# One power for rows of x1 and scale of u, and a new order of steps on GpSimd and VectorE

## The reference

```python
xn = layernorm(x)
x1 = x + gnn(xn, edges) + mix(xn)      # gnn: softmax over 4 heads, gathered rows; mix: attention in a hyperbolic ball
y  = x1 + ffn(layernorm(x1))           # ffn: a router picks 2 of 8 experts for all rows, then layernorm
# mix, per block of rows, where one batch row makes each attention its own position:
#   t = relu(bn(xn @ w_qkv)), s = pointwise(t), q, k = relu, v; out = (v k) q / (v + 1e-15)
#   scaled by norms of t, s and out; u = out @ w_res + b; fx = tanh(|u|) u / |u|, clipped at the ball's edge
```

## Time and profile before

| | |
|---|---|
| time, median of 3 runs | 835.66 us (833.97 to 837.52) |
| profiled execution, its own time | 833.71 us |
| its span | 831.9 us |
| attention stage with its tail, 218 to 486 us | 268.0 us |
| TensorE busy, share of the span | 94% |
| VectorE / ScalarE / GpSimd busy | 63% / 51% / 46% |

### The profile page before, as it was taken

How to read it: one execution, slowest core, us unless ns; L and a number is a source line. 1 busy time by engine, 2 the same in 40 slices (tenths; PEclk the granted TensorE clock), 3 DMA queues, 4 the chain that set the end, 5 groups by cost and what they waited for, 6 DMA issues and landing times. The chain is left out here.

```text
span 831.9 us, 15073 instructions
## 1 busy us (share of the span) xinstructions
PE 780.0 (94%) x5042; PEld 639.1 (77%) x5042; DVE 525.7 (63%) x1480; ACT 424.9 (51%) x963; POOL 384.8 (46%) x601
## 2 busy tenths in 40 slices
PE   5899999999798999999669899999999999999996
PEld 3778888888466666666446788888888888888885
DVE  6863488797578888888988635353535353535345
ACT  2566436889679888888657242323222222223230
POOL 2430878878068888877646502221213131313122
PEclk9999999999999999999979999999999999999999
DMA  9855122222011110211100040000000000000000
GB/s 216 208 146 148 43 57 57 51 57 52 8 50 47 51 59 25 63 45 53 41 10 30 20 126 14 26 13 25 13 25 13 25 12 25 16 23 17 22 20 30
DMA packets 35420, 41.31 MB, mean 50 GB/s; under 512 B 11520, under 2 KB 20696, under 8 KB 35339
## 3 DMA queue, kind: packets, MB, share of 16 engines
q1 hardware_dynamic: 22355, 30.71, 12.9%
q0 software_dynamic: 8000, 6.82, 3.8%
q10 hardware_dynamic: 4984, 2.79, 1.4%
HBM read 25.59 MB, written 14.60 MB: 48 GB/s over the span
## 5 line engine op out<-in xcount | busy, mean ns | idle before, releaser
L926 ACT ACTIVATE Z<-ps,b1s 128x250 f32<-128x250 f32 x200 | 93.5, 469 | 233.1 <-PE ps L1195 233.1
L1208 PE MATMUL ps<-Z 128*125 128x256 f32 x800 | 176.5, 379 | 0.0
L1195 PE MATMUL ps<-Z 128*128 128x250 f32 x800 | 173.3, 374 | 0.4 <-DMA Z<-in_w 0.4
L1208 PEld LDWEIGHTS ps<-Z 128*125 128x125 f32 x800 | 150.1, 188 | 22.3
L1195 PEld LDWEIGHTS ps<-Z 128*128 128x128 f32 x800 | 151.4, 189 | 18.3 <-DMA Z<-in_w 0.6
L988 PE MATMUL ps<-Z,L 128*128 128x250 f32 x600 | 126.9, 373 | 0.0
L655 POOL TENSOR_SCALAR zr<-zmv 125x1 f32<-125x1 f32 x50 | 11.1, 221 | 249.2 <-issue 239.9
L988 PEld LDWEIGHTS ps<-Z,L 128*128 128x128 f32 x600 | 113.6, 189 | 13.2
L1794 DVE TENSOR_TENSOR Z<-ps,L 125x256 f32<-125x256 f32 x50 | 21.2, 424 | 160.2 <-PE ps L1208 159.9
L1110 PE MATMUL ps<-wr,Z 128*125 128x256 f32 x400 | 92.6, 384 | 0.0
L780 ACT ACTIVATE Z<-Z,bn_o,bn_s 128x250 f32<-128x250 f32 x150 | 80.7, 598 | 1.5 <-DVE bn_o L1495 1.5
(11 more groups left out here) (221 smaller groups left out, 1274.0 us busy)
## 6 DMA issues: line engine op xcount, KB each, us to landing
Z<-in_x SPq DMA_DIRECT2D x25, 250.0 KB
out<-Z SPq DMA_DIRECT2D x24, 250.0 KB
xt_table<-L SPq DMA_DIRECT2D x25, 231.0 KB
Z<-in_x SPq DMA_DIRECT2D x1, 2016.0 KB
g_table<-gt SPq DMA_DIRECT2D x25, 62.5 KB
gr<-g_table SPq DMA_DIRECT2D x25, 62.5 KB
Z<-in_x SPq DMA_DIRECT2D x1, 1344.0 KB
Z<-in_w SPq DMA_DIRECT2D x2, 512.0 KB, 3.3
```

Source lines behind the costliest of these rows:

```text
L926: a_.activation(ge[:, b % 2, f, :], ps[:, f % 4, 0:BT], ACT.Gelu, bias=b1s[:, f // NF, f % NF:f % NF + 1]).then_inc(gelu_done.sem, 1)
L1195: last = mm(ps[:, f % 4, 0:BT], w1s[:, f // NF, k, (f % NF) * 128:(f % NF + 1) * 128], h_of(b, k), start=(k == 0), stop=(k == KD - 1))
L1208: last = mm(ps[0:TP, 4 + 2 * (b % 2) + t, 0:D], ge[:, b % 2, f, t * TP:(t + 1) * TP], w2s[:, f // NF, f % NF, :], start=(f == 0), stop=(f ...
```

## The change

GpSimd: two powers of a step, one of two columns for the rows of x1 of block s-3 and one of two columns for u of block s-2, become one of four columns (`powers`), which stands where the second stood and therefore waits for the moments of x1 and for the squares of u. Its inputs and results lie in new small tiles `pin` and `rsu`. The flag goes ahead of the last scale of u, and the gather goes from the end of the step to behind the scale of the norms. In the three steps behind the loop the powers stay apart. VectorE: `check_t` and the branch go ahead of `make_x1`. The router's small tile `rt` moves into space of the big tile Z that is free by then. Waits of ScalarE and of later readers follow the new names.

```diff
+            def powers(k, rows_=True, u_=True):
+                a = k % 2
+                if rows_:
+                    wait_apart(pool, x1, x1.count(k - 1))
+                    g.tensor_scalar(pin[0:TP, a, 0], mv2[0:TP, k - 1, :, 1], LN_EPS, None, ALU.add).then_inc(var_made.sem, 1)
+                if u_:
+                    wait_apart(pool, u_sq, u_sq.count(k))
+                    g.tensor_scalar(pin[0:TP, a, 1], us[0:TP, a], MIN_NORM ** 2, None, ALU.max).then_inc(sq_made.sem, 1)
+                if rows_:
+                    pool.wait_ge(var_made.sem, var_made.count(k - 1))
+                if u_:
+                    pool.wait_ge(sq_made.sem, sq_made.count(k))
+                js = slice(0 if rows_ else TB, 2 * TB if u_ else TB)
+                powered = rows_pow if rows_ else u_pow
+                g.tensor_tensor(rsu[0:TP, k].rearrange("p r t -> p (r t)")[:, js], pin[0:TP, a].rearrange("p r t -> p (r t)")[:, js],
+                                nhalf[0:TP, js], ALU.pow).then_inc(powered.sem, 1)
             def scale_of_u(b):
-                s, n = sg[0:TP, b % 2], scale_g
                 if b >= 2:
                     pool.wait_ge(x1.sem, x1.count(b - 2))
-                wait_apart(pool, u_sq, u_sq.count(b))
-                g.tensor_scalar(s[:, 0], us[0:TP, b % 2], MIN_NORM ** 2, None, ALU.max).then_inc(n.sem, 1)
-                pool.wait_ge(n.sem, n.count(b, 1))
-                g.tensor_tensor(s[:, 1], s[:, 0], nhalf[0:TP, 0:TB], ALU.pow).then_inc(n.sem, 1)
-                pool.wait_ge(n.sem, n.count(b, 2))
-                g.tensor_tensor(s[:, 2], s[:, 0], s[:, 1], ALU.mult).then_inc(n.sem, 1)
+                pool.wait_ge(*made_of_u(b))
+                g.tensor_tensor(sg[0:TP, b % 2, 0], pin[0:TP, b % 2, 1], rsu[0:TP, b, 1], ALU.mult).then_inc(scale_g.sem, 1)
...
-            def rstd_of_x1(b):
-                wait_apart(pool, x1, x1.count(b))
-                g.tensor_scalar(vr[0:TP, b % 2], mv2[0:TP, b, :, 1], LN_EPS, None, ALU.add).then_inc(rstd_done.sem, 1)
-                pool.wait_ge(rstd_done.sem, rstd_done.count(b, 1))
-                g.tensor_tensor(rstd2[0:TP, b], vr[0:TP, b % 2], nhalf[0:TP, 0:TB], ALU.pow).then_inc(rstd_done.sem, 1)
             steps(NB, [
+                (1, raise_flag),
                 (3, last_scale_of_u),
-                (1, raise_flag),
                 (1, scale_of_norms),
+                (2, gather_piece),
                 (2, lambda b: add_edge(b) if b >= 2 else None),
-                (3, rstd_of_x1),
+                (2, lambda b: powers(b, rows_=b > 0)),
                 (2, scale_of_u),
-                (2, gather_piece),
                 (2, lambda b: add_edge(b) if b < 2 else None),
             ])
...
             def make_xn(b):
-                dve.wait_ge(rstd_done.sem, rstd_done.count(b))
+                dve.wait_ge(rows_pow.sem, rows_pow.count(b))
...
             steps(NB, [
-                (3, make_x1),
                 (0, check_t),
                 (1, divide_where_needed),
+                (3, make_x1),
                 (3, sums_of_x1),
```

More of the change, by code:

```diff
@@ L138, in gps_layer @@
         mv2 = sb("mv2", [128, NB, TB, 2])
-        rstd2 = sb("rstd2", [128, NB, TB])
+        pin = sb("pin", [128, 2, 2, TB])
+        rsu = sb("rsu", [128, NB + 1, 2, TB])
         rsum = sb("rsum", [128, KD, NB])
@@ L158, in gps_layer @@
         us = sb("us", [128, 2, TB])
[L159 to L160 removed]
+        sg = sb("sg", [128, 2, 4, TB])
         st2 = sb("st2", [128, TB, 6])
@@ L226, in gps_layer @@
         yo = take(2 * TB * D).rearrange("p (a t d) -> p a t d", a=2, t=TB)
+        rt = take(19 * (EX + 1))[0:1].rearrange("p (i e) -> p i e", i=19)
         take = cut((0, LW, L))
@@ L341, in gps_layer @@
         u_sq = stage("u_sq", TB)
-        scale_g = stage("scale_g", 5)
+        scale_g = stage("scale_g", 3)
         tanh_done = stage("tanh_done", 1)
         x1 = stage("x1", 3 * TB)
-        rstd_done = stage("rstd_done", 2)
+        var_made = stage("var_made", 1)
+        sq_made = stage("sq_made", 1)
+        u_pow = stage("u_pow", 1)
+        rows_pow = stage("rows_pow", 1)
         xn_made = stage("xn_made", TB)
@@ L368, in gps_layer, with made_of_u @@
         passed = {e.engine: sem(f"passed{i}") for i, e in enumerate((nc.vector, nc.gpsimd))}
+        def made_of_u(b):
+            if b in (0, NB - 2, NB - 1):
+                return u_pow.sem, u_pow.count(max(0, b - (NB - 3)))
+            return rows_pow.sem, rows_pow.count(b - 1)
         def wait_apart(eng, stg, value):
@@ L616, in last_scale_of_u @@
                 wait_apart(pool, tanh_done, tanh_done.count(b))
[L617 to L625 removed]
+                g.tensor_scalar(s[:, 2], s[:, 1], MAXNORM, None, ALU.min).then_inc(n.sem, 1)
+                pool.wait_ge(n.sem, n.count(b, 2))
+                g.tensor_tensor(s[:, 3], s[:, 2], rsu[0:TP, b, 1], ALU.mult).then_inc(n.sem, 1)
             steps(NB, [
+                (1, raise_flag),
                 (3, last_scale_of_u),
[L629 removed]
                 (1, scale_of_norms),
+                (2, gather_piece),
                 (2, lambda b: add_edge(b) if b >= 2 else None),
[L632 removed]
+                (2, lambda b: powers(b, rows_=b > 0)),
                 (2, scale_of_u),
[L634 removed]
                 (2, lambda b: add_edge(b) if b < 2 else None),
             ])
+            raise_flag(NB - 1)
             last_scale_of_u(NB - 3)
[L638 removed]
             scale_of_norms(NB - 1)
             add_edge(NB - 2)
[L641 removed]
+            powers(NB - 2, u_=False)
+            powers(NB - 2, rows_=False)
             scale_of_u(NB - 2)
@@ L645, in _ @@
             add_edge(NB - 1)
+            powers(NB - 1, rows_=False)
             scale_of_u(NB - 1)
             last_scale_of_u(NB - 1)
-            rstd_of_x1(NB - 2)
-            rstd_of_x1(NB - 1)
+            powers(NB - 1, u_=False)
+            powers(NB, u_=False)
             def z_scale(n):
@@ L1638, in make_x1 @@
                 for t in range(TB):
-                    v_.scalar_tensor_tensor(out=x_of(b, t), in0=u[0:TP, b % US, t], scalar=sg[0:TP, b % 2, 5, t:t + 1],
+                    v_.scalar_tensor_tensor(out=x_of(b, t), in0=u[0:TP, b % US, t], scalar=sg[0:TP, b % 2, 3, t:t + 1],
                                             in1=x_of(b, t), op0=ALU.mult, op1=ALU.add).then_inc(x1.sem, 1)
```

13 lines of the change are left out of this document (5 added, 8 removed).

## The result

| | before | after |
|---|---|---|
| median on the same chip | 836.59 us (833.97 to 838.79, 4 runs) | 848.29 us (846.95 to 849.73, 4 runs) |
| ratio, with its 95% interval | 1 | 1.0143 (1.0119 to 1.0167) |
| profiled execution, its span | 831.9 us | 847.1 us |
| its own time | 833.71 us | 848.88 us |

The account below looks back on a forecast made before the run. TensorE was taken to bound the loop at 8.92 us a step. Flag -2.2, ring +0.5 and taken branch +0.5 gave -1.2 us, a median of 834.5 from 835.66; own range 832.5 to 837, with rivals 829.5 to 840.5.

Parts of the forecast that it names:

- x1 behind the branch: VectorE, attention loop: x1 ends about where it did, cost nothing; up to 0.9 us in steps with the pause if cover fails.
- the power's ring: Loop from the end of L1567 through flag, scales, gather, edge sum, power of four and `make_xn` to the next L1567.
- the pause of 0.90 us: VectorE's pause between x1 with the check and the branch in some steps, expected to fall ahead of x1 instead.
- charged it to five steps: `gprod` stretches L617 from 0.23 to 0.52 us in five late-product steps with a gather, making the ring 9.1 us.
- The ring fits under TensorE with 0.12 us to spare.: Loop: the ring sums to 8.80 us against TensorE's 8.92 a step; cost 0.5 us for all, bounds 0 and 1.5.
- the rival of the long ring: Loop: ring longer than 8.92 us, each 0.1 costing 2 us over some 20 steps; at 9.2 us, 840; chance 0.20.
- the signs of being wrong that I had named: L1563 never waiting for TensorE or even steps of 9.1 us or more; steps 7, 11, 15 at 8.92; taken branch over 1.5 longer.
- The flag, "gain 2.2 us": GpSimd, loop: flag 0.9 us earlier, so `fixed` comes earlier and waits shrink; gain 2.2 us, bounds 0 and 5.
- The power, "worth nothing by itself; its price is the order": GpSimd, loop: one power saves about 0.4 us per step of idle time, worth nothing; x1's reciprocals come later.
- The taken branch, "a loss of 0.5 us, between a gain of 0.6 and a loss of 2": Step 21: flag 0.5 to 0.9 us earlier, but x1 behind the long body and gather beside its copies; loss 0.5 us.
- The rule on descriptor generation: VectorE beside the gather: by the skill, L1624 with two SBUF inputs is left alone; otherwise it waits up to 1.35 us.

Follow-up runs that it names:

- E11: The changed kernel with x1 moved between the check and the branch; 843.91 us, ratio 1.0079 to the kernel before.
- E3: The changed kernel with x1 ahead of the check and the branch again, single power kept; 835.50 us, ratio 1.0011 to the kernel before.
- E8: The changed kernel with two powers and x1 first again, leaving only the flag and gather edits; 836.07 us, ratio 1.0004 to the kernel before.
- E5: The kernel before with one edit, x1 behind the check and the branch; 852.87 us, ratio 1.0199.
- E1: The changed kernel with the gather put back to the end of GpSimd's step; 847.52 us, ratio 1.0151 to the kernel before.
- E12: The kernel before with one edit, the check ahead of x1 and the branch behind x1; 840.63 us, ratio 1.0048.
- E10: The changed kernel with a check reading v once, no tiny-t test and the branch never taken; ratio 0.9861 to the kernel before, only steps compare (9.49 us).
- E9: The kernel before with one edit, one power of four columns in place of two; 842.57 us, ratio 1.0080.
- E2: The changed kernel with two powers of two columns instead of one of four; 840.05 us, ratio 1.0061 to the kernel before.
- E6: The kernel before with one edit, the gather behind the scale of the norms; 838.35 us, ratio 1.0030.
- E13: The changed kernel with two powers and x1 between the check and the branch; 839.86 us, ratio 1.0033 to the kernel before.

## Why the prediction was wrong

**Where the 12 us are.** Taken apart in one order, by the sums of steps 5 to 20 (after 156.9, E11 153.4, E3 148.0, E8 145.9, before 146.8 us): x1 behind the branch costs 3.5 us in these steps, the check beside the flag 5.4, the single power 2.1, and flag and gather win 0.9. In step 21 the branch ahead of x1 costs 3.2 more, of which 2.5 us lie behind TensorE's wait, where its clock is low (below). These are differences between single traces. In the times E11 and E3 differ clearly (ratios 1.0079 and 1.0011), and so do after and E11 (1.0143 and 1.0079); the 2.1 us of the power (E3 and E8, 1.0011 and 1.0004) and the 0.9 us of flag and gather (E8 and before) are below what the times can tell. The parts depend on the order: on the kernel before, x1 behind the branch costs 13 us by itself (E5), because there the flag is late; that after the early flag hides some of it, and the power's ring, already full, the rest, is how I read it.

**"x1 behind the branch. I take nothing for it."** This is the step that failed. I reasoned that the pause of 0.90 us would move ahead of x1 and the flag come 0.9 us earlier, so that x1 would end where it did. The flag did come early, 0.26 us behind L1587 on average. But before, x1 did not wait for the flag at all: it started with the end of the last scale of u, 0.04 us behind the flag's start. Behind the branch it starts 1.7 to 1.8 us after it (means of after, E1 and E5: 1.72, 1.81 and 1.66), and with the check as only cover VectorE is idle for the whole of it in E5 (35.4 us in 19 steps) and for about half of it in after (12.9 us in 14). The bound that I gave, up to 0.9 us, was taken from a pause that had both x1 and the check ahead of it; the whole way from flag to the first instruction behind the branch was the term to be priced. Two runs bear this out: with x1 first again (E3) the whole loss is gone, and with the branch behind x1 (E12) 0.70 of E5's 0.82 us per step are gone. What is more, the order put the check where x1 had been, beside the flag and the last scale of u, and it has two SBUF inputs, as `gprod` has. I had seen and charged it to five steps; x1's move made it every step.

**"The ring fits under TensorE with 0.12 us to spare."** The second failed step, and the rival of the long ring in fact, with a chance of 0.20 and a price of 840 us. The terms, as means over the same 16 rounds (u's input is that of the power, L622):

| | worked out | E3 | after |
|---|---|---|---|
| end of L1567 to flag | 0.20 | 0.26 | 0.26 |
| flag and last scale of u | 0.87 | 1.07 | 1.38 |
| scale of the norms and gather | 3.41 | 3.46 | 3.43 |
| edge sum | 1.50 | 1.51 | 1.52 |
| to the start of u's input | 0.31 | 0.37 | 0.45 |
| u's input and power, to `make_xn` | 1.39 | 1.54 | 1.69 |
| `make_xn` to end of L1567 | 1.12 | 1.04 | 1.01 |
| sum | 8.80 | 9.25 | 9.74 |

This was a ring of the kernel after, and not the only one (E1, E5). Its durations were right too, but the pauses between two small instructions of GpSimd (0.08 to 0.13 us in E3's rows where I added durations, and 0.15 ahead of the power, which waits for its own input) make it 8.99 in the steps without late work and 9.25 as a mean with them. That alone brings it to TensorE's 8.92 and costs E3 nothing over before. The other half microsecond of after is the check (0.31, E10 and E11) and 0.23 us around the power, where one of its inputs or the power itself lies beside L1564 (0.61 us for L619 in the step shown, 0.23 in E3). That last piece I only read from the rows; no run takes L1564 away. That rival priced a ring of 9.2; with 9.81 for 9.18, sixteen steps cost 10.1 us, and that is why even its 840 was too low. Two of the signs of being wrong that I had named came: L1583 waits for TensorE in none of the steps 5 to 21, and the taken branch is longer by over 1.5 us.

**The flag, "gain 2.2 us".** Right in mechanism: every wait of ScalarE for the end of the branch outside step 21 is gone, L1587 is not held up by the gather, and steps 2 to 4 alone are 2.0 us shorter. In E8, where nothing else binds, it comes to 2.3 us over steps 2 to 20 of the trace; in the time no gain shows (1.0004). In after the rings bind, and it is not seen in steps 5 to 20.

**The power, "worth nothing by itself; its price is the order".** The first half is too kind: alone it costs 0.8% (E9), as it makes GpSimd wait for the squares of u with gather, scale and flag queued behind it. In after the wait is covered in most steps (6.3 us in six steps is left), and the price is that of the ring, 2.1 us with x1 first (E3 against E8) and 16 x 0.41 = 6.6 with x1 behind the branch (after against E2).

**The taken branch, "a loss of 0.5 us, between a gain of 0.6 and a loss of 2".** It lost 4.7. Two rows of the body after, and GpSimd beside them:

```profile
418.40 0.16 DVE L1604 TENSOR_TENSOR et<-nrm,npw 125x2 f32<-125x2 f32 x1 [1.06 <-POOL npw L596]
...
419.82 1.76 DVE L1614 COPY L<-L 64x128 f32<-64x128 f32 x1
```

```profile
419.38 1.35 POOL L575 DMA_INDIRECT xg<-xt_table,idst  x1 [0.29 <-issue]
```

The same copy took 0.22 us before:

```profile
409.65 0.22 DVE L1594 COPY L<-L 64x128 f32<-64x128 f32 x1
```

That copy is one term, 1.5 us, which I had named and priced at less. It starts 0.44 us behind the gather and outlasts it by 0.85 us, into the edge sum that follows at 420.77. With it `fixed` comes late, and TensorE waits 16.4 us instead of 14.2. TensorE goes on at 434.59 (before, 422.86), and step 22 starts 7.81 us behind that (before, 5.34). These 2.5 us and the 2.2 us of wait are the 4.7 us. Two stretches after (us, busy time and instructions of PE, PEld, DVE, ACT, POOL, granted clock, DMA share, GB/s):

```profile
434.00:443.00 9.00, 8.11 (x72) 3.75 (x76) 6.72 (x19) 3.94 (x12) 1.77 (x4) 0.52 0.01 2
443.00:452.00 9.00, 8.97 (x100) 5.81 (x96) 6.35 (x19) 8.17 (x20) 4.95 (x11) 1.00 0.08 20
```

And the stretch from the same event to step 22 before:

```profile
422.80:428.20 5.40, 5.34 (x61) 2.95 (x61) 4.79 (x13) 3.27 (x10) 2.25 (x5) 0.70 0.01 3
```

Read in slices of half a microsecond, the clock is 0.50, its lower level of 1.2 GHz, when TensorE goes on, in both kernels. Before, it is back at 1.00 some 3 us later, and the 0.70 of the row is a mean of both levels; after, it takes 8 us. By TensorE's busy time, 8.11 us at 0.52 is some 4.2 us of work at full speed and 5.34 at 0.70 some 3.7: 3.9 us go to the clock after, against 1.6 before, 2.3 us more, which is nearly all of the 2.5.

It is not the length of the wait that sets how long the clock stays low. Behind 15.7 us of wait in E11 and 15.4 in E3 it was low for about 3 us, behind 14.9 in E1 for about 6, and behind 15.7 in E6 for about 5.5. What does set it no run shows. No row of before gives a price for it. E6's 2.6 us in step 21 are 1.4 of wait and 1.1 behind it, E11's 1.5 us are all wait, and E5 has no longer wait than before (14.0 us): most of the longer wait comes with the gather.

**The rule on descriptor generation.** L1644 (L1624 before), the first instruction of `make_u`, has two SBUF inputs and now lies beside the gather. In after it took 0.16 us in nearly all steps and 0.78 once:

```profile
303.19 0.78 DVE L1644 SCALAR_TENSOR_TENSOR se<-npw,cc 125x2 f32<-125x2 f32 x1
```

```profile
302.85 1.35 POOL L575 DMA_INDIRECT xg<-xt_table,idst  x1 [0.20 <-issue]
```

That looks like the rule, by which the gather leaves it alone, but it is only where L1644 happens to fall. The twelve that took 0.13 or 0.16 us beside a gather had started within 0.31 us of the gather's start; the one shown started 0.34 us behind it and ended 1.12 us behind it. In E3, where L1644 starts 0.37 to 0.89 us behind the gather's start, 17 of 18 were held: they took 0.22 to 0.75 us, and each ended 1.11 to 1.13 us behind that start. E6, E8, E11 and E13 show the same, with one exception in each as in E3. So the gather does hold a VectorE instruction with two SBUF inputs, until 1.1 us into its 1.35. The sentence that the prediction took from the Trainium skill, SBUF — State Buffer, "Who interferes with whom", that descriptor generation needs the write interface (the page calls it inferred), does not fit these rows, and the measurement decides. It did not change the forecast: before, the same instruction lay beside the edge sum and took 0.32 to 0.74 us in most steps. The copy above, which has one input, was held too; this fits the same section of the Trainium skill, by which copies can enter a mode that takes the port pair that GpSimd shares.

## What to carry to other kernels

Before an instruction goes behind a data-dependent branch, price the whole way from the start of what raises the flag to the first instruction behind the branch, and ask what that instruction waited for before; here it was 1.7 us against nothing. A ring of dependences that comes out within 2% of the bound from durations alone should be summed from starts of neighbouring instructions, since small instructions leave 0.1 us between them, and each must be looked at for what the other engine runs beside it in the new order. Where several edits move one step, try each alone and each left out: here one of them carried a loss larger than the whole, and two that cost 0.3 and 0.4% alone showed no cost together. An instruction that looks untouched beside another engine's work may only have started early enough: look at a run in which it starts later.

## What the runs showed of the hardware

- From the start of the flag on GpSimd to the first VectorE instruction behind a branch that is not taken, 1.5 to 1.9 us pass in the steps shown, though the flag itself takes 0.37.
- A VectorE instruction over 128x500 with two SBUF inputs beside GpSimd's flag stretches it from 0.37 to 0.60 us, and beside the last scale of u L643 from 0.20 to 0.48 us. The same check with one input stretches neither (E10). `gprod`, 125x512 with two inputs, stretches L641 from 0.23 to 0.55 us.
- An indirect gather's issue (1.35 us) left a VectorE instruction of 125x2 with two SBUF inputs alone where that started within 0.31 us of the gather's start (0.16 us), and held it until 1.11 to 1.13 us behind that start where it started at 0.34 us or later (17 of 18 in E3).
- A VectorE copy of 64x128 beside the same issue and the start of the edge sum took 1.76 us instead of 0.22, and 1.36 us in E3, where it started later.
- Behind waits of TensorE of 14 to 16 us the granted clock was 0.50 and came back to 1.00 after about 3 us (14.2 us of wait, before; 15.7, E11), 6 us (14.9, E1) or 8 us (16.4, after): the length of the wait alone does not tell.
